# New places in the instruction lists of ScalarE, VectorE and GpSimd in a one-core transformer layer

## What is computed

```python
x = x + attn_a(layernorm(x))   # 16 heads of 128, causal softmax attention, biases, output projection
x = x + ffn(layernorm(x))      # int8 rows: q = round(xn / scale), q @ weight.T * scale * w_scale + bias
x = x + attn_b(layernorm(x))   # 16 heads, rotary q and k, 64 slots, cumulative log-sum-exp,
                               # two causal products, RMS norm, gate g * sigmoid(g), projection
x = x + ffn(layernorm(x))
```

## Time and profile before

| | before |
|---|---|
| median of three runs | 781.54 us (780.91 to 783.22) |
| profiled execution | 783.86 us, of which the span 782.1 us |
| busy: PE, its weight loads | 97%, 82% of the span |
| busy: VectorE, ScalarE, GpSimd | 75%, 63%, 50% |
| mean granted clock of TensorE | 0.989 |
| DMA | 43.38 MB, mean 55 GB/s |

### The profile page before, as it was taken

How to read it: one execution, slowest core, us unless ns; L and a number is a source line. 1 busy time by engine, 2 the same in 40 slices (tenths; PEclk the granted TensorE clock), 3 DMA queues, 4 the chain that set the end, 5 groups by cost and what they waited for, 6 DMA issues and landing times.

```text
span 782.1 us, 13097 instructions
## 1 busy us (share of the span) xinstructions
PE 756.9 (97%) x4470; PEld 643.3 (82%) x4470; DVE 585.6 (75%) x1474; ACT 490.8 (63%) x1289; POOL 389.4 (50%) x372
## 2 busy tenths in 40 slices
PE   8999999999999998999999999999999999999995
PEld 6888888888888887788887878888888888788883
DVE  4655546556655656789899898888898998889877
ACT  3765566665666676566767756756666666666632
POOL 4544224323233424456656676645656665774522
PEclk9999999999999999999999999999999999999997
DMA  7223211121111122111111202102111120210100
GB/s 233 81 59 90 68 56 55 55 65 58 54 54 55 55 68 68 41 41 54 43 40 55 67 16 67 55 15 68 54 42 41 55 68 15 62 61 15 41 1 27
DMA packets 43909, 43.38 MB, mean 55 GB/s; under 512 B 4114, under 2 KB 43538, under 8 KB 43716
## 3 DMA queue, kind: packets, MB, share of 16 engines
q1 hardware_dynamic: 43844, 42.55, 17.4%
HBM read 41.49 MB, written 1.05 MB: 54 GB/s over the span
## 4 chain that ended last, share of the span: by engine, by line
PE 85%; DVE 7%; ACT 5%; issue 2%; DMA 1%; POOL 1%; SPq 0%; ACTq 0%; DVEq 0%
PE ps L1541 22%; PE ps L1735 10%; PE ps L1617 7%; PE ps L1548 5%; PE ps L1574 5%; PE ps L1622 3%; PE ps L1751 3%; PE ps L1599 3%; PE ps L1582 2%; PE ps L1778 2%; PE ps L1764 2%; PE ps L1798 2%; PE ps L1797 2%; PE ps L1796 2%; PE ps L1752 2%; PE ps L1600 2%
## 5 line engine op out<-in xcount | busy, mean ns | idle before, releaser
L429 POOL TENSOR_TENSOR w_lo<-w_raw,w_hi 128x512 fp32r<-128x512 f32 x64 | 81.5, 1286 | 76.3 <-ACT w_hi L651 75.4
L1541 PE MATMUL ps<-xT_hi,w_hi 128*128 128x512 f32 x256 | 109.4, 427 | 3.7 <-ACT rot_s L819 2.8
L1541 PE MATMUL ps<-xT_hi,w_lo 128*128 128x512 f32 x256 | 100.7, 393 | 0.0
L1541 PE MATMUL ps<-xT_lo,w_hi 128*128 128x512 f32 x256 | 100.4, 392 | 0.0
L501 POOL TENSOR_TENSOR rot_s<-rot_s,const 128x512 f32<-128x512 f32 x64 | 82.2, 1294 | 22.7 <-ACT rot_s L819 22.7
L1228 DVE TENSOR_TENSOR wt<-ps,const 128x384 f32<-128x384 f32 x128 | 67.9, 553 | 25.5 <-PE ps L1781 12.1
L429 POOL TENSOR_TENSOR wc_lo<-wv,wc_hi 128x512 fp32r<-128x512 f32 x16 | 20.4, 1278 | 104.0 <-ACT wc_hi L651 104.0
L1112 DVE TENSOR_TENSOR v<-ps,bv_b 128x256 f32<-128x256 f32 x64 | 27.0, 423 | 54.1 <-PE ps L1548 54.1
L728 ACT ACTIVATE wt<-wt,negmax 128x128 f32<-128x128 f32 (+1 forms) x128 | 56.8, 446 | 15.5 <-DVE negmax L1124 15.5
L1216 DVE RECIPROCAL enz<-zs 128x128 f32<-128x128 f32 x64 | 60.4, 944 | 0.0
L1541 PEld LDWEIGHTS ps<-xT_hi,w_hi 128*128 128x128 f32 x256 | 48.4, 189 | 13.5 <-ACT rot_s L819 3.1
(11 more groups left out here) (199 smaller groups left out, 2333.5 us busy)
## 6 DMA issues: line engine op xcount, KB each, us to landing
w_raw<-a_w_q SPq DMA_DIRECT2D x16, 256.0 KB, 3.0
w_raw<-a_w_k SPq DMA_DIRECT2D x16, 256.0 KB, 3.8
wv<-a_w_v SPq DMA_DIRECT2D x16, 256.0 KB, 2.7
wo<-a_w_o SPq DMA_DIRECT2D x16, 256.0 KB, 2.7
w_raw<-b_Wq SPq DMA_DIRECT2D x16, 256.0 KB, 2.7
w_raw<-b_Wk SPq DMA_DIRECT2D x16, 256.0 KB, 3.1
wc<-b_Wv SPq DMA_DIRECT2D x16, 256.0 KB, 2.7
wc<-b_Wg SPq DMA_DIRECT2D x16, 256.0 KB, 3.0
```

Of the source, the lines that this page charges most:

```text
L429: g.tensor_tensor(lo[:, :, :], raw[:, :, :], hi[:, :, :].bitcast(F32), ALU.subtract).then_inc(ph.w_lo, 1)
L1541: ins = mm(PJ[bank], w[:, m, c, h * P:(h + 1) * P], x[:, c, cols], start=(t == 0), stop=(t == len(terms) - 1))
```

## The change

Nothing is added to the arithmetic or taken from it; instructions change their place in their engine's list.

- **GpSimd:** in B8, B9, B24 and B25 the FFN tail moves from ahead of the slots to the end of the list: behind k0's product with the sines in even steps, behind the last weights' low part in odd ones.
- **ScalarE:** in A22 the two roundings move from the end of the step to a new place 3, right behind the output copy (in stage B they stay at place 2). In odd steps of stage A the output copy moves between the exponentials of head 0 and head 1. In A30 the exponentials move behind q1, the output copy and z; in A31 k1 moves ahead of both weight copies.
- **VectorE:** in r = 9 the second output scaling moves from place 0 to place 1 (behind the maxima in A25, behind the scores' masks in B9 and B25). In r = 6 the scalings of the second sequence move from place 2 to place 3 (behind the maxima in A22; in B6 and B22 from ahead of q0's cosine product to behind a reciprocal, ahead of q0's rotary addition). In A30 and A31 the low part of the output moves ahead of the rotary additions of q0 and q1, both of these ahead of the normalisation, and the first two reciprocals `b_recip` further back.

```diff
--- before.py
+++ after.py
@@ -591,14 +591,19 @@
                     rms(x)
                     rope_mul(ahead, "q0", 0, 0)
                     rope_mul(ahead, "q1", 0, 1)
-                    portion(0, 1, x)
-                    portion(1, 0, x - PHASES)
+                    if x % 16 not in (8, 9):
+                        portion(0, 1, x)
+                        portion(1, 0, x - PHASES)
                     slots(x + 1)
                     rope_mul(ahead, "k0", 1, 0)
+                    if x % 16 in (8, 9):
+                        portion(0, 1, x)
+                        portion(1, 0, x - PHASES)
                 else:
                     rope_mul(ahead, "k1", 1, 1)
-                    portion(0, 1, x)
-                    portion(1, 0, x - PHASES)
+                    if x % 16 not in (8, 9):
+                        portion(0, 1, x)
+                        portion(1, 0, x - PHASES)
                     rms(x)
                     split_out_tail(b_, phase, wos)
                     if ahead + 1 < PHASES:
@@ -700,12 +708,12 @@
                         s1_copy(half)
                 if place == 1 and r == 12 and f == 0:
                     transposed(1, b + 1, 7)
+                if r == 6 and place == (3 if (f, half) == (0, 0) else 2):
+                    ffn_round(f, b)
+                    ffn_round(f, b + 1)
                 if place == 2:
                     if r == 3:
                         row_scale(2 * f + 1, half)
-                    if r == 6:
-                        ffn_round(f, b)
-                        ffn_round(f, b + 1)
                     if r == 11 and f == 0:
                         row_scale(2, half)
 
@@ -720,8 +728,8 @@
                 bias = (bqs, bk)[m][:, head:head + 1]
                 s.activation(dst, PJ[bank], ACT.Identity, bias=bias, scale=(SCALE, 1.0)[m]).then_inc(a.proj_evac[bank], 1)
 
-            def a_exp_step(x):
-                for h in range(2):
+            def a_exp_step(x, heads=(0, 1)):
+                for h in heads:
 
                     act.wait_ge(a_max, 2 * x + h + 1)
                     for r, (lo, hi) in enumerate(((0, P), (P, 3 * P))):
@@ -760,6 +768,7 @@
                     portion(0, 0, x - PHASES, 1)
                     a_exp_step(x + 1)
                     out_copy(a, a.o_ps, x)
+                    portion(0, 0, x - PHASES, 3)
                     a_qk(ahead, 2)
                     a_qk(ahead, 3)
                     for m in range(2):
@@ -775,8 +784,9 @@
                     weights_copy(x, 1)
                     portion(0, 0, x - PHASES, 0)
                     a_out_weights(phase)
-                    a_exp_step(x + 1)
+                    a_exp_step(x + 1, (0,))
                     out_copy(a, a.o_ps, x)
+                    a_exp_step(x + 1, (1,))
                     portion(0, 0, x - PHASES, 2)
 
             split_head(a, 0, 0)
@@ -931,14 +941,14 @@
             weights_copy(x, 1)
             b_task(0, "s")
             b_task(0, "q0")
-            a_exp_step(x + 1)
             b_task(0, "q1")
             out_copy(a, a.o_ps, x)
             b_task(0, "z")
+            a_exp_step(x + 1)
             b_task(0, "k0")
+            b_task(0, "k1")
             x = LAST
             weights_copy(x, 0)
-            b_task(0, "k1")
             weights_copy(x, 1)
             b_task(0, "c0")
             a_out_weights(PHASES - 1)
@@ -1070,8 +1080,10 @@
                 b, ph = 2 * half, (a, b_)[f]
                 if r == 1 and place < 2:
                     add_rows(ph, b + place)
-                if r == 9 and place == 0:
+                if r == 9 and place == 1:
                     ffn_out(f, b + 1)
+                if r == 6 and place in (2, 3):
+                    ffn_scale(f, b + place - 2, half + 1)
                 if r == 13 and place == 1 and f == 0:
                     s1_tail(half)
                 if r == 12 and place == 3 and f == 0:
@@ -1082,9 +1094,6 @@
                         ln_stats(2 * f + 1, b + 1, ph.fin_acc, b + 2)
                     if r == 4:
                         ffn_range(f, slice(4 * half, 4 * half + 4), 4 * half + 4, half + 1)
-                    if r == 6:
-                        ffn_scale(f, b, half + 1)
-                        ffn_scale(f, b + 1, half + 1)
                     if r == 8:
                         ffn_out(f, b)
                     if r == 10 and f == 0:
@@ -1287,6 +1296,7 @@
                     b_rope_cos(ahead, "q1")
                     b_recip(ahead, 0)
                     portion(0, 1, x, 3)
+                    portion(1, 0, r, 3)
                     b_rope_add(ahead, "q0")
                     b_okn_max(x + 1)
                     b_rope_add(ahead, "q1")
@@ -1327,18 +1337,18 @@
             b_rope_cos(0, "q0")
             a_max_step(x + 1)
             b_rope_cos(0, "q1")
+            out_tail(a, x)
             b_rope_add(0, "q0")
+            b_rope_add(0, "q1")
             a_norm_step(x + 1)
-            out_tail(a, x)
-            b_recip(0, 0)
-            b_rope_add(0, "q1")
             b_rope_cos(0, "k0")
             add_group(a, x)
-            b_recip(0, 1)
+            b_recip(0, 0)
             x = LAST
             b_rope_cos(0, "k1")
             b_rope_add(0, "k0")
             b_rope_add(0, "k1")
+            b_recip(0, 1)
             b_gate(0, 0)
             b_gate(0, 1)
             out_tail(a, x)
```

## The result

The changed kernel takes 774.34 us (median of five runs, 773.53 to 774.47), the kernel before, in five runs, 782.93 us (780.91 to 783.22): a ratio of 0.989 (95% interval 0.988 to 0.9901). It is faster by 8.6 us; the forecast was 771.9, or 9.6 us, with a range of 769.0 to 776.5. Of the 2.4 us above the forecast 1.4 come from the kernel before, whose median of three runs had been 781.54, and 1.0 from the gain. The profiled execution of the changed kernel took 773.53 us, its span is 771.7 us at a mean clock of 0.994.

A forecast was written before the change was run, and what follows sets the result against it. PE bounds the kernel (busy 756.9 of 782.1 us), so only its idle or slow-clock time can be won. 5.0 + 1.6 + 2.5 - 0.6 + 0.4 + 0.7 = 9.6 us; 781.54 - 9.6 = 771.9, range 769.0 to 776.5.

The forecast's parts named there:

- A30 and A31: Steps A30, A31: earlier copies shorten PE's wait before k0, keep the clock up and end c1's wait; 5.0 us won.
- Rival 2: A30's gain is given back in A31, or the clock falls again: 2.5 us in place of 5.0, 774.4; chance 0.14.
- The output copy: Odd stage A steps: earlier copy ends the output product's weight-load wait; ten steps at 0.25, 2.5 us won.
- rival 1: Odd stage A steps: the output copy gives nothing, or the "issue" wait has another cause; 774.4, chance 0.14.
- Rival 4: Odd stage A steps: head 1's exponential comes late behind the output copy and holds both heads; slower, 786.4, chance 0.04.
- Rounding in A22: Earlier roundings end PE's wait ahead of A23's FFN transposes; 1.6 us won, bounds 1.3 and 1.7.
- A25: Later output scaling delays GpSimd's FFN tail, whose second addition holds VectorE's normalisation; 0.6 us lost.
- rival 3: GpSimd's addition in A25 follows the normalisation, and B9's additions miss the rotation: 0.85 and 1.5 more won, 769.6; chance 0.14.
- B6 and B22: Two scalings leave the masks' path; PE is early there but waits for the next slots; 0.2 us a step, 0.4 won.
- B8 to B10: FFN tail moved behind slots and k0: 0.35 us won from B8's slots to B10's, twice, 0.7 in all.
- PE waiting at step starts in stage B for over a microsecond: Sign of a wrong forecast: GpSimd's tail would hold more than was counted.

The follow-up runs named there:

- experiment 2: Kernel before with only the output copy of odd stage A steps moved between the two heads' exponentials: 779.78 us, ratio 0.9963.
- experiment 8: Changed kernel with the output copy of odd steps ahead of both heads' exponentials: 780.02 us, ratio 0.9972 to the kernel before.
- experiment 3: Kernel before with only the A22 roundings and the r = 6 scalings moved: 779.47 us, ratio 0.9964.
- Experiments 5: Changed kernel with VectorE's squares of the slots' sums in B10 and B26 moved behind masks and reciprocal: 772.65 us, ratio 0.988 to the kernel before.
- experiments 9: Changed kernel with A25's second output scaling back at place 0 and the squares of B10 and B26 on ScalarE: 772.60 us, ratio 0.9869 to the kernel before.
- 10: Changed kernel with GpSimd's FFN tail back ahead of the slots in B9 and B25 alone: 782.63 us, ratio 1.0004 to the kernel before.

## Why the prediction was right, and where not

**A30 and A31: right in sum and mechanism.** 4.97 us of 5.0, with the clock at 1.00 and the forecast wait of 0.3 before k0 (0.30). Rival 2 is out: A31 won its 0.86, and c1 waits no more.

**The output copy: right.** 0.235 a step over ten steps, where 0.25 stood; no gain in A3 and A5, as was read from the held normalisation in the earlier trace rows. Reading the 13 "issue" waits as waits for the copy was an inference; experiment 2 shows it, and rival 1 is out. Rival 4 is a true price (6.0 us in experiment 8, 6.9 expected) for a place that the change didn't take.

**Rounding in A22: right mechanism, 0.34 too small.** The 1.6 us of the forecast were the first wait, which gave 1.63. It did not see the second one, for the second rounding, inside the 0.92 us of the transposes (0.30, experiment 3); so the 1.94 lie above its bound of 1.7.

**A25: right.** 0.55 us lost of 0.6 forecast, by the addition and the instruction named. The first half of rival 3 is out.

**B6 and B22: right, small.** 0.29 in place of 0.2 a step. The wait of 0.62 us is gone, and a wait of 0.19 for the following step's slots is new (L1816, at the starts of B7 and B23), as the forecast had it.

**B8 to B10: the step that failed.** Two things were priced, the steps up to B10's slots (0.35 won) and what comes behind (nothing). The first was better than forecast: 0.54 and 0.51 us. The second cost 0.74 and 0.77. The prediction had the tail's time right, behind the last low part and so at the start of B10, had the rule that a two-input instruction of VectorE stands still beside such an addition, and went through the rotations of 128x512 with it. For B10 it asked only who waits for GpSimd (low part, cumulative sums, statistics), not which of VectorE's instructions run beside the addition. The one it missed has four columns and takes 0.2 us; with it the term of +0.7 became -0.46, 1.16 of the difference. Experiments 5, 9 and 10 part the square from the addition in three ways, and each time B26 comes back to its length of before; B10 does so in experiments 9 and 10. The other terms add +0.4 (0.34 + 0.18 + 0.05 - 0.15 - 0.03). So 9.6 - 1.16 + 0.39 = 8.83, the steps' sum; that the total lies so near the forecast is in part luck, since these misses go both ways.

The second half of rival 3, that the additions in B9 miss the rotation, is out: the first addition holds k0's rotation, as the forecast had it.

```profile
445.39 1.29 POOL L466 TENSOR_TENSOR y<-y,fb_b 128x512 f16<-128x512 f32 x1
445.55 1.68 DVE L1211 TENSOR_TENSOR kT<-rot,rot_s 128x512 f32<-128x512 f32 x1
```

The point "PE waiting at step starts in stage B for over a microsecond would mean that GpSimd's tail holds more than I counted" named the right place; 0.89 us was already that sign.

## What to carry over

When work is moved on GpSimd's list, write down all that VectorE does in the new stretch, the smallest instructions too: here one of four columns with two inputs in SBUF paid the rest of GpSimd's instruction and not its own size, and all behind it was late. An instruction that has no good place beside a busy GpSimd may have one on another engine (0.22 us on ScalarE). A merged row can hide a wait: the one of eight transposes held a second wait, which only the weight loads show. Before one of several edits is undone alone, see whether a second one needs it: the tail's place and the scaling's place are one edit (5.1 us a step).

## What was not expected of the hardware

A VectorE instruction of 128x4 that took 0.16 to 0.35 us elsewhere took 1.13 and 1.68 us beside GpSimd's additions, in both cases up to 0.03 us behind the end of GpSimd's instruction; the profile shows this as busy time of VectorE, not as a wait.
